# Softmax division moved from attention's blocks to the tail, the shift shared with GpSimd, and routing placed at attention's head

## The reference

```
xn = layernorm(x)
x  = x + linear_attention(xn) + fp6_linear(xn)       # layer 0: 8 heads, windows of 32
xn = layernorm(x)
x  = x + attn_block(xn) + moe(xn)                    # layer 1
attn_block: y  = softmax(rope(q) rope(k)^T / sqrt(16)) v   over 16 heads of 16
            r  = xn + y Wo + bo
            r + relu(layernorm(r) W1 + b1) W2 + b2
moe:        shared gelu MLP + the two best of 8 experts for each token, weighted
            by their shares of the softmax over the experts
```

## Time and profile before

| | |
|---|---|
| Time, median of 3 runs | 4616.81 us (4616.56 to 4619.07) |
| Profiled execution, on the device | 4626.26 us |
| its span, first to last instruction | 4624.5 us |
| Front | 0 to 598 us |
| Routing | 598 to 622 us, DVE busy 17.1 |
| Attention, maxima of block 0 | 622 to 750 us |
| Attention, blocks | 750 to 3540 us |
| Experts | 3540 to 4134 us, DVE busy 60, PE 563 |
| Tail | 4134 to 4624.5 us, DVE busy 103, PE 486 |
| TensorE busy, whole span | 4221.0 us (91%) |
| VectorE busy | 3267.1 us (71%) |
| ScalarE busy | 2670.8 us (58%) |
| GpSimd busy | 409.1 us (9%) |

### The profile page before, as it was taken

One profiled execution on the slowest core, in us unless ns is written; L12 is line 12 of the kernel. 1 busy time (PEld: TensorE's weight loads), 2 busy tenths in 40 slices (PEclk: granted clock), 3 DMA queues, 4 the chain that ended last, 5 costly groups with the idle time before them and its releaser, 6 DMA issues. The chain is left out here.

```text
span 4624.5 us, 70156 instructions
## 1 busy us (share of the span) xinstructions
PE 4221.0 (91%) x23643; PEld 1849.4 (40%) x23944; DVE 3267.1 (71%) x5315; ACT 2670.8 (58%) x5129; POOL 409.1 (9%) x370
## 2 busy tenths in 40 slices
PE   6888725999999999999999999999998899999999
PEld 3665501222222222222222222222223788876666
DVE  6877557999999999999999999999990011112111
ACT  4445302777777777777777777777776222222222
POOL 1233464000000000000000000000000100011110
PEclk8989856999999999999999999999999999999999
DMA  4222356000001200001300000000002755531111
GB/s 144 74 92 78 105 115 157 12 3 4 3 3 24 55 2 4 2 3 22 57 3 4 2 3 4 2 3 4 3 3 92 244 192 191 191 121 61 53 51 37
DMA packets 216336, 256.22 MB, mean 55 GB/s; under 512 B 39408, under 2 KB 187120, under 8 KB 214416
## 3 DMA queue, kind: packets, MB, share of 16 engines
q1 hardware_dynamic: 206064, 221.64, 16.6%
q0 software_dynamic: 9888, 30.04, 2.1%
HBM read 180.57 MB, written 70.78 MB: 54 GB/s over the span
## 5 line engine op out<-in xcount | busy, mean ns | idle before, releaser
L1199 DVE TENSOR_REDUCE a_MX<-a_MP 128x1 f32<-128x512 f32 x4096 | 2631.5, 685 | 144.9 <-PE a_MP L1073 84.2
L1171 ACT ACTIVATE a_PT<-a_ST 128x512 f32<-128x512 f32 x4096 | 2108.4, 605 | 810.4 <-PE a_ST L1092 519.3
L1106 PE MATMUL a_OT<-a_PT,a_VG 128*32 128x512 f32 x8192 | 1093.9, 606 | 1.2 <-ACT a_PT L1171 0.9
L1092 PE MATMUL a_ST<-a_QS,a_KS 128*128 128x512 bf16 x3795 | 1033.4, 383 | 56.9 <-ACT a_PT L1171 23.6
L1073 PE MATMUL a_MP<-a_KS,a_QS 64*128 64x512 bf16 x4096 | 817.0, 396 | 153.8 <-DVE a_MX L1199 105.7
L1073 PEld LDWEIGHTS a_MP<-a_KS,a_QS 64*128 64x128 bf16 x4096 | 196.9, 93 | 1403.3 <-DVE a_MX L1199 1341.0
L1092 PEld LDWEIGHTS a_ST<-a_QS,a_KS 128*128 128x128 bf16 x4096 | 319.9, 98 | 551.4 <-ACT a_PT L1171 279.3
L1398 ACT ACTIVATE e_hT<-e_up,e_BF 128x256 f32<-128x256 f32 x312 | 147.9, 474 | 411.8 <-PE e_up L1351 411.7
L1351 PE MATMUL e_up<-e_xT,e_WF 128*128 128x256 f32 x1248 | 323.9, 383 | 0.8 <-DVE e_xT L1408 0.8
L1360 PE MATMUL e_dn<-e_WP,e_hT 128*128 128x256 f32 x1248 | 321.9, 381 | 0.0
L1106 PEld LDWEIGHTS a_OT<-a_PT,a_VG 128*32 128x32 f32 x8192 | 161.4, 108 | 235.9 <-ACT a_PT L1171 215.9
(11 more groups left out here) (220 smaller groups left out, 2820.8 us busy)
## 6 DMA issues: line engine op xcount, KB each, us to landing
e_WF<-Wfc SPq DMA_DIRECT2D x39, 1024.0 KB, 5.0
e_WP<-Wproj SPq DMA_DIRECT2D x39, 1024.0 KB, 7.1
a_QS<-scr_qparts SPq DMA_DIRECT2D x384, 32.0 KB, 7.4
a_KS<-scr_kparts SPq DMA_DIRECT2D x48, 256.0 KB, 11.8
scr_xs<-f_zero SPq DMA_DIRECT2D x1, 9984.0 KB, 33.0
e_XS<-scr_xs SPq DMA_DIRECT2D x39, 256.0 KB, 2.7
scr_ys<-e_Y SPq DMA_DIRECT2D x39, 256.0 KB, 2.1
f_X<-x SPq DMA_DIRECT2D x16, 512.0 KB, 4.6
```

The source lines that it names most:

```text
L1092: T.matmul(ST[:, c % SBANKS, :], KS[j][:, h, u * P:(u + 1) * P], QS[j][:, bass.ds((b * HG + h) * BLK, BLK)], start=True, stop=True).then_i ...
L1106: last = T.matmul(OT[w, :], VG[j][:, u, w], PT[:, (HG * u + h) % RING, :], start=u == 0, stop=u == KT - 1)
L1171: nc.scalar.activation(PT[:, c % RING, :], ST[:, c % SBANKS, :], ACT.Exp, scale=SOFT_SCALE).then_inc(S["exp_done"], 1)
L1199: V.reduce_max(MX[:, side, x:x + 1], bank(e + side), AX.X).then_inc(S["mp_free"], 1)
```

## The change

Attention: the transposes of OS, `normalise` and the tiles rd and AO go. SyncE stores OS itself, sums and all, to `scr["att"]`, now laid out by feature, and ScalarE's copy waits for the store of the block before. Of the shift VectorE keeps the reduce; GpSimd does the three operations of the split, behind its row scatter; the maxima get two buffers. Only block 0's shift stays as it was.

Routing: `route` is gone as a stage. Its operations stand at the head of each engine's stream in attention, ahead of what attention did first; its tiles lie in the ring PT, its two counts in the score banks. The two small loads stand ahead of group 0's. GpSimd makes tri and ones before its memsets, and waits for the slots before it scatters.

Tail: a block loads, for each group, the sums' numerators of 64 features (SUM) and the denominators, repeated over 16 partitions (DEN): 11 DMAs in place of 4. VectorE takes the reciprocal and multiplies (`attended`) into attT: block 0's in the last tiles of the experts, block i+1's in block i after Z. The transposes and copies of ATT go.

```diff
+        "att": dram("att", (NG, P, N_TOK)),
     }
 
...
-        gt = [sb(f"gt{i}", [P, NT, NE]) for i in range(5)]
-        g1s = [sb(f"g1s{i}", [P, NT]) for i in range(3)]
...
 TURN_MAX = 29
-EVENTS = SIDES * PAIRS + 2
+EVENTS = SIDES * PAIRS + 1
 HEAD_EVENTS = SIDES * (PAIRS + LEAD) + 1
 RING = 12
+SHIFT_STEPS = 2
 SOFT_SCALE = float(HD1) ** -0.5
...
-        MX = sb("MX", [P, SIDES, PAIRS])
+        MX = [sb(f"MX{j}", [P, SIDES, PAIRS]) for j in range(2)]
...
-        rd = sb("rd", [P, TPB, HG])
-        AO = sb("AO", [P, TPB, HG * HD1])
...
+
+        ring = PT[:].rearrange("p r n -> p (r n)")
...
+        def part(*shape):
...
+            ends[0] = a + size
+            v = ring[:, a:a + size]
+            return v.rearrange("p (a b) -> p a b", b=shape[1]) if len(shape) == 2 else v
...
+        gt = [part(NT, NE) for _ in range(5)]
...
+            nc.gpsimd.memset(tri, 1.0).then_inc(S["tchain"], 1)
+            pool.wait_ge(S["tchain"], 1)
+            nc.gpsimd.affine_select(out=tri, in_=tri, compare_op=ALU.is_gt, fill=0.0, base=0,
+                                    pattern=[[1, P]], channel_multiplier=-1).then_inc(S["tri_ok"], 1)
+            nc.gpsimd.memset(ones, 1.0).then_inc(S["tri_ok"], 1)
+            pool.wait_ge(S["tri_ok"], 2)
+            def shifts(n):
+
+                G = nc.gpsimd
+                at = [0]
+
+                def step(ins):
+                    at[0] += 1
+                    ins.then_inc(S["shift"], 1)
+                    pool.wait_ge(S["shift"], (n - 1) * SHIFT_STEPS + at[0])
+
+                pool.wait_ge(S["maxed"], n)
+                sides = neg[:].rearrange("p (s c) -> p s c", s=SIDES)
+                step(G.tensor_copy(negparts[:, :, 0, :], sides))
+                step(G.tensor_tensor(sides, sides, negparts[:, :, 0, :], ALU.subtract))
+                G.tensor_copy(negparts[:, :, 1, :], sides).then_inc(S["negmax_ready"], 1)
...
-            nc.gpsimd.memset(OS[:], 1.0).then_inc(S["pchain"], 1)
-            pool.wait_ge(S["pchain"], 3)
+            pool.wait_ge(S["ident_ok"], 1)
...
             pool.wait_ge(S["ones_ok"], 4 * SIDES)
+            pool.wait_ge(S["slots_ok"], TOPK)
...
             for j in range(2):
                 pool.wait_ge(row_store[j], NB // 2 * TPB * TOPK * 16)
+            for n in range(1, NG * NB):
+                shifts(n)
...
             def store_out(n, G, b):
-                sp.wait_ge(S["normed"], n + 2 + 1)
-                sp.dma_start(scr["att"][bass.ds(b * BLK, BLK), G * HG * HD1:(G + 1) * HG * HD1].rearrange(
-                    "(t p) c -> p t c", p=P), AO[:]).then_inc(S["att_store"], 16)
-
+
+                sp.wait_ge(S["o_copied"], n + 2)
+                sp.dma_start(scr["att"][G, :, bass.ds(b * BLK, BLK)], OS[:]).then_inc(S["att_store"], 16)
+
+            sp.dma_start(flat(idxkey), io["idxkey"].partition_broadcast(P)).then_inc(S["num_load"], 16)
+            sp.dma_start(flat(num), io["tilenum"].partition_broadcast(P)).then_inc(S["num_load"], 16)
             load_group(0)
             load_group(1)
             sp.wait_ge(S["ones_ok"], 4 * SIDES)
...
-            def out_transpose(e, n):
-                room(e)
-                pe.wait_ge(S["o_copied"], n + 1)
-                for t in range(TPB):
-                    last = T.transpose(bank(e)[:, t * P:(t + 1) * P], OS[:, t * P:(t + 1) * P], identf[:])
-                last.then_inc(S["mp_full"], 1)
...
-                            if u == TURN_OUT:
-                                out_transpose(e, n)
-                                e += 1
...
+            pe.wait_ge(S["tri_ok"], 2)
+            pe.wait_ge(S["both_ok"], 1)
+            T.matmul(ST[:, 0, 0:NT * NE], tri, flat(both), start=True, stop=True).then_inc(S["counted"], 1)
+            T.matmul(ST[:, 1, 0:NT * NE], ones, flat(both), start=True, stop=True).then_inc(S["counted"], 1)
             pe.wait_ge(S["first"], FIRST * 16)
...
-            out_transpose(first_event(NG * NB - 1) + 1, NG * NB)
...
+            act.wait_ge(S["gate_in"], 1)
+            nc.scalar.activation(gt[1], gt[0], ACT.Exp).then_inc(S["gate_out"], 1)
...
-                act.wait_ge(S["mp_full"], HEAD_EVENTS + n * EVENTS + (SIDES * (2 * TURN_OUT + 1) if more else -SIDES * LEAD) + 1)
+                act.wait_ge(S["att_store"], n * 16 + 1 + 16)
                 nc.scalar.copy(OS[:], OT[:]).then_inc(S["o_copied"], 1)
...
+            r = Chain(dve, S["rchain"])
+            r.step(V.tensor_reduce(g1s[0], LG[:], AX.X, ALU.max))
+            V.tensor_tensor(gt[0], LG[:], bcast(g1s[0], NE), ALU.subtract).then_inc(S["gate_in"], 1)
+            dve.wait_ge(S["num_load"], 32)
+            dve.wait_ge(S["gate_out"], 1)
...
+            dve.wait_ge(S["counted"], 2)
+            r.step(V.tensor_copy(run[0], count))
+            for k, d in enumerate(ROUTE_STEPS):
+                a, b = run[k % 2], run[1 - k % 2]
+                r.mark(V.tensor_copy(b[:, 0:d, :], a[:, 0:d, :]))
+                r.step(V.tensor_tensor(b[:, d:NT, :], a[:, d:NT, :], a[:, 0:NT - d, :], ALU.add))
...
+            r.step(V.tensor_scalar(tiles[0], upto[:, NT - 1, :], 1.0 / ET, (ET - 1.0) / ET - 0.498, ALU.mult, ALU.add))
+            r.step(V.tensor_scalar(tiles[0], tiles[0], 2.0 ** 23, None, ALU.add))
+            r.step(V.tensor_scalar(tiles[0], tiles[0], -2.0 ** 23, None, ALU.add))
+            r.step(V.tensor_copy(first, tiles[0]))
...
+            for k in range(TOPK):
+                r.step(V.tensor_tensor(sel, place, pick[k], ALU.mult))
+                r.step(V.tensor_reduce(slotf, sel, AX.X, ALU.add))
+                V.tensor_copy(slot[:, k, :], slotf).then_inc(S["slots_ok"], 1)
+                dve.wait_ge(S["slots_ok"], k + 1)
...
+            r.step(V.tensor_copy(owner[:], ownf))
             c = Chain(dve, S["chain"])
...
-            def maximum(e, x):
+            def maximum(n, e, x):
                 for side in range(SIDES):
                     dve.wait_ge(S["mp_full"], e + side + 1)
-                    V.reduce_max(MX[:, side, x:x + 1], bank(e + side), AX.X).then_inc(S["mp_free"], 1)
-
...
+                    last = V.reduce_max(MX[n % 2][:, side, x:x + 1], bank(e + side), AX.X).then_inc(S["mp_free"], 1)
+                return last
...
+                                dve.wait_ge(S["mp_free"], e + MBANKS)
+                                V.tensor_reduce(neg[:], MX[(n + 1) % 2][:].rearrange("p s (c k) -> p (s c) k", k=KB), AX.X, ALU.max,
+                                                negate=True).then_inc(S["maxed"], 1)
...
-                        if x == 2 * TURN_OUT:
-                            normalise(n, e)
-                            e += 1
...
-                c.step(V.reciprocal(rd[:], o4[:, :, :, HD1]))
-                dve.wait_ge(S["att_store"], n * 16 + 1)
-                V.tensor_tensor(AO[:].rearrange("p t (h e) -> p t h e", h=HG), o4[:, :, :, 0:HD1],
-                                bcast(rd[:], HD1), ALU.mult).then_inc(S["normed"], 1)
...
+                if j < DC:
+                    if j == 0:
+                        dve.wait_ge(*rows_load(tt, 0))
+                    attended(dve, V, tt, 0, j)
+
+
+TAIL_IN = 3 + 2 * NG
...
-    for name, src in (("ATT", "att"), ("XN1", "xn1"), ("RES", "resid")):
+    for G in range(NG):
+        rows, k = slice(G % 2 * HALF, (G % 2 + 1) * HALF), G // 2
+        heads = scr["att"][G].rearrange("(h w) n -> h w n", h=HG)
+        eng.dma_start(tt["SUM"][j][rows, k, :], heads[:, 0:HD1, n]).then_inc(there, 16)
+        eng.dma_start(tt["DEN"][j][rows, k, :], heads[:, HD1:HD1 + 1, n].to_broadcast([HG, HD1, BLK])).then_inc(there, 16)
+    for name, src in (("XN1", "xn1"), ("RES", "resid")):
         eng.dma_start(tt[name][j][:], scr[src][n, :].rearrange("(t p) c -> p t c", p=P)).then_inc(there, 16)
     eng.dma_start(tt["xT"][j][:], scr["xn1T"][:, n].rearrange("(c p) n -> p c n", p=P)).then_inc(there, 16)
...
+def attended(dve, V, tt, i, k):
+
+    j = i % 2
+    V.reciprocal(tt["DEN"][j][:, k, :], tt["DEN"][j][:, k, :]).then_inc(tt["att_chain"], 1)
+    dve.wait_ge(tt["att_chain"], i * DC + k + 1)
+    V.tensor_tensor(tt["attT"][:, k, :], tt["SUM"][j][:, k, :], tt["DEN"][j][:, k, :], ALU.mult).then_inc(tt["att_ready"], 1)
...
-            def turn_att(i):
-                pe.wait_ge(*rows_load(tt, i))
-                for k in range(DC):
-                    turn(ATT[i % 2], k, use_att(i, k))
...
-                pe.wait_ge(S["a_drained"], use_att(i, DC - 1) + 1)
+                pe.wait_ge(tt["att_ready"], (i + 1) * DC)
...
+                if u == 0:
+                    pe.wait_ge(*rows_load(tt, i))
...
-            turn_att(0)
             pe.wait_ge(tt["w_load"], TAIL_W * 16)
...
-                    if u == TURN_ATT and i + 1 < NB:
-                        turn_att(i + 1)
...
-            def copy_att(i):
-                for k in range(DC):
-                    use = use_att(i, k)
-                    act.wait_ge(S["a_filled"], use + 1)
```

(13 more changed lines are left out.)

200 lines of the change are left out of this document (66 added, 134 removed).

## The result

The changed kernel takes 4569.1 us (median of four, 4567.2 to 4570.2), the one before in the same comparison 4617.75: a ratio of 0.9895, 95% interval 0.988 to 0.991, so 48.7 us or 1.05% less. In a second session it was 4583.3 against 4624.8; the ratio on record there is 0.9899 (0.9883 to 0.9915), that of the two medians 0.9910. The forecast was 4563, from 4530 to 4586. The profiled execution took 4568.3 us on the device, its span is 4566.5.

The account below looks back on a forecast made before the run. TensorE was taken to set the pace in attention, VectorE just behind. Attention -52, head +4, experts +3 and tail -8.8 sum to -54 us, so median 4616.8 becomes 4563, range 4530 to 4586.

Parts of the forecast that it names:

- Division and shift: In each attention block: removing transposes and division gains 1.0 us, splitting the shift with GpSimd 0.6.
- The term of attention: Attention's blocks and end: 1.6 us in each of 31 blocks plus small end gains, -52 us, bounds -30 and -55.
- its loss stays: At a block's head: weights wait behind ScalarE's copy of OS; that wait was taken as untouched, its loss unchanged.
- Routing at the head: Attention's head: routing moved inside makes the first maximum 21 us later, 17 comes back; +4, bounds -6 and +22.
- The hold: In routing: GpSimd's memsets hold VectorE's one-input operations, one passing between any two; first maximum near 664 us, 21 later.
- overlap of 68 us: Block 0: scatter overlap falls from 68 us to 26, stalls in proportion from 27 to 10, so 17 come back.
- rival B: Attention's head: memsets hold routing and nothing comes back from block 0's stalls; head +21, 4580 us; chance 0.11.
- Experts and tail: Experts: larger early loads cost +3 us, bounds 0 and +6. Tail: transposes and copies gone, -8.8, bounds -6 and -9.
- A: Attention's head: memsets hold nobody, head gives -21.8 us and block 0's stalls stay; 4537 us; chance 0.15.
- C: Attention's blocks: VectorE's pace nearer TensorE's, a new wait replaces the old, 26 us less gain; 4589 us; chance 0.07.
- D: Shift in attention's blocks: GpSimd's chain becomes late, kernel slower, 4643 us at a 13 us chain; chance 0.03.
- E: Attention block's head: TensorE takes its time back behind ScalarE, so nothing changes; about 4615 us; chance 0.03.

Follow-up runs that it names:

- session C: Repeat session on another chip: kernel before again 4626.9 us, changed kernel again 4583.3 us (0.990), plus variants of the changed kernel.
- session B: Session on a chip of its own with four variants of the changed kernel, 4541.3 to 4571.4 us; the kernel before had median 4604.3 us.

## Why the prediction was right, and its step that failed

*Division and shift.* Both places measured what the sum had: 1.01 and 0.62 us. The shift and the transposes are also shown by putting them back. The term of attention was still too large, 44.8 us from first to last copy where 48.3 were foretold. The step that failed is the sentence on ScalarE's copy, that "its loss stays". It grew: the pause was 2.08 us in the mean and is 2.22, and 30 blocks of 0.13 are 4 us, where 3.5 are missing. It grew in every variant with the loop, with the shift on either engine and the store early or late. What the new loop body does to the load of its code is open. The pause as a whole is 1.5 us of each block (45.1 by 30), about what the change's two edits in attention came to together.

*Routing at the head.* The hold was foretold from one row of an operation that reads the earlier trace rows and came for fills as well, one operation let through between two. F to the first maximum is +20.6 for +21. The absolute time, 664, was missed (652.8) because this execution's front was 11 us shorter.

*Block 0.* -14.8 for -18.6, and -10.0 in session C. (The prediction's overlap of 68 us is 66 by its own rows.) The stalls followed the overlap in three sessions: over 86.8 us (88.4 before the change, an estimate from 86.8 and the 1.6 of the block) the block took 25, 12, 23, 14 and 29 us more with 66, 29, 66, 27 and 78 us of scatter beside it, 0.34 to 0.53 for each. But it was a reading of one execution taken for a trait of the kernel. In the other two sessions the block takes 86.8 to 89.8 us in every kernel, and nothing can come back: there the move costs 19.4 us at the head and 17.4 in the medians, 4571.4 against 4553.9 in session B (the one with the store late, the other with routing by itself), and rival B's mechanism is what happens. The kernel with the store late gained 32.9 us there on the kernel before, where the prediction had 54. That the forecast came within 6 us is in this part luck: the time was taken where the stalls exist, and in the profiled execution the front was the shortest of fourteen.

*Experts and tail.* +3.0 and -8.7, for +3 and -8.8. The experts' figure agrees by chance as much as by size: in session C the same two kernels give +6.1 (576.4 and 582.5), the changed kernel and its variants with the same experts took 576.3 to 582.5 us, and the stall grew by 1.5 us in the first pair and 4.9 in the second, for 2.9. The tail's holds: its blocks stand 59.42 us apart instead of 60.30.

*The sum.* The profiled execution of before lay 9.5 us above its median, and the prediction carried that over without asking where it sat. The segments of -58 include -10.9 in the untouched front; without it they give -47.1, and the medians -48.7. The front took 587.6 to 606.6 us in fourteen profiles of the same code. In one stretch of it the granted clock, a mean over stretches at 2.4 and at 1.2 GHz, was 0.94 of full speed after and 0.87 before (two windows, the first of the changed kernel; columns as in the earlier trace rows). That it makes the whole 11 us was not tried.

```profile
240.00:300.00 60.00, 50.54 (x346) 34.82 (x346) 48.47 (x64) 30.50 (x59) 21.93 (x16) 0.94 0.25 82
```

```profile
240.00:300.00 60.00, 53.03 (x344) 38.64 (x343) 45.67 (x65) 28.65 (x54) 22.09 (x20) 0.87 0.22 71
```

*The rivals.* A fell with the held copies. B fell in the first session and in C, and is what session B shows. C and D fell: the one bracket before PE's pairs in the middle of a block is the 0.35 us behind the turn of the shift, which the kernel before had too, and POOL's chain takes 0.8 us where 10.4 are free. E had its place right, ScalarE at the block's head, and its sign: 0.13 us, not 1.6.

## What to carry to other kernels

Cut both spans at the same marks before a difference is explained, and subtract what lies in stages that the change doesn't touch. When work is moved beside another engine's, ask which of its operations the neighbour can hold: here the same fills cost some 40 us on GpSimd (F + 65.1 for the first maximum, against 25.4) and held nothing on ScalarE. A pause that recurs at the end of a loop's body, with a releaser that had long been done, is worth one run with the loop written out before any operation around it is shaved.

## What the runs showed of the hardware

- A memset of 6.9 us on GpSimd held VectorE's copies, casts and tensor_scalars from SBUF to SBUF until its end, and let one start between two fills: six in a row in the changed kernel, two in the kernel with the fills behind the slots. Beside other fills of the same series tensor_reduce and tensor_tensor (0.42 us), reciprocal (0.35) and a copy from PSUM (0.42) ran at their usual length. The Trainium skill (SBUF — State Buffer, Who interferes with whom) names the first three as holders of the shared ports and clears tensor_reduce; the rows agree.
- A back edge in ScalarE's loop costs 2.05 to 2.4 us, of which 1.5 reached the block (45.1 us by 30).
- GpSimd's row scatter (loads of rows and indirect writes) slowed block 0 by 12 to 29 us in three sessions and by at most 3 in two, on other chips; no view names what VectorE waits for in the gaps.
- The same front took from 588 to 607 us.
